# Interleaving 32 DRAM-to-DRAM weight conversions with the weight loads of an early projection, on eight cores

## The reference, cut to what matters

```python
xn = _layernorm(x)                                  # x: (4, 4096, 1024) f32
# attention-like part, D = 1024
magnitude = sigmoid(xn @ W_mag.T + b_mag) * 5.0
phi = random_phases * position * 0.01
mem_r = cumsum(magnitude * xn * cos(phi), axis=1)   # over all 4096 positions
mem_i = cumsum(magnitude * xn * sin(phi), axis=1)
acc_mag = cumsum(magnitude, axis=1)
q_off = xn @ W_q.T + b_q
... retrieved_r, retrieved_i from mem_r, mem_i, acc_mag, phi + q_off
context = concat([xn * cos_phi, xn * sin_phi, retrieved_r, retrieved_i])
attn = xn + (gelu(layernorm(context) @ W1.T + b1) @ W2.T + b2)
# feed-forward part, hidden width 4096
h = silu(xn @ w1.T * s1) * (xn @ w2.T * s2)
h = gelu(h @ h1_w.T * h1_s)                         # 4096 x 4096
h = gelu(h @ h2_w.T * h2_s)                         # 4096 x 4096
ffn = h @ w3.T * s3
return x + attn + ffn
```

## Time and profile before

| | us |
|---|---|
| median of two runs | 4950.73 |
| lowest and highest of them | 4926.67 and 4974.8 |
| the profiled execution | 4914.08 |
| its span, slowest core (core 1) | 4912.4 |
| spans of the eight cores | 4886.4 to 4912.4 |
| PE busy in the span | 3552.7 (72%) |
| DVE busy | 1630.9 (33%) |
| ACT busy | 925.0 (19%) |
| POOL busy | 399.9 (8%) |

### The profile page before, as it was taken

How to read it: one execution, slowest core, us unless ns; L and a number is a source line. 1 busy time by engine, 2 the same in 40 slices (tenths; PEclk the granted TensorE clock), 3 DMA queues, 4 the chain that set the end, 5 groups by cost and what they waited for, 6 DMA issues and landing times.

```text
span 4912.4 us, 46625 instructions; the slowest of 8 cores (4886.4 to 4912.4 us)
## 1 busy us (share of the span) xinstructions
PE 3552.7 (72%) x15504; PEld 1540.9 (31%) x15504; DVE 1630.9 (33%) x3773; ACT 925.0 (19%) x1243; POOL 399.9 (8%) x756
## 2 busy tenths in 40 slices
PE   3342002035879999878799997887999878899993
PEld 3220001002333444233244432332444333344441
DVE  2365667860023440430334405212443061100003
ACT  2111002220113331101133311011332200111000
POOL 0002001000120000001100000011000000210000
PEclk9997556557999999799899998998999899999997
DMA  2248994996684444376744444776444366844443
GB/s 75 77 107 101 110 120 55 110 109 117 113 137 131 148 149 151 69 142 115 118 146 152 152 131 79 149 114 122 150 153 154 95 113 136 124 145 152 154 140 79
DMA packets 125701, 600.90 MB, mean 122 GB/s; under 512 B 15867, under 2 KB 15900, under 8 KB 78364
## 3 DMA queue, kind: packets, MB, share of 16 engines
q0 software_dynamic: 108288, 545.31, 53.2%
q1 hardware_dynamic: 17180, 52.60, 3.3%
HBM read 866.29 MB, written 75.50 MB: 192 GB/s over the span
## 4 chain that ended last, share of the span: by engine, by line
PE 58%; DMA 19%; DVE 13%; issue 7%; ACT 2%; DVEq 1%; SPq 0%; POOLq 0%; ACTq 0%
PE ps L505 46%; DMA wstage<-w_t 9%; DMA wstage<-fw_t 5%; PE ps L985 2%; PE ps L976 2%; DMA xo<-pos_p 2%; PE ps L701 2%; PE ps L880 1%; DVE xo L473 1%; PE ps L870 1%; DMA xo<-x_fm 1%; DMA wstage<-h2b 1%; DMA wstage<-wq_t 1%; DVE big L477 1%; PE ps L331 1%
## 5 line engine op out<-in xcount | busy, mean ns | idle before, releaser
L505 PE MATMUL ps<-big,wstage 128*128 128x512 bf16 x12032 | 2691.9, 386 | 351.0 <-DMA wstage<-w_t 142.5
L505 PEld LDWEIGHTS ps<-big,wstage 128*128 128x128 bf16 x12032 | 1181.7, 99 | 1864.3 <-issue 524.2
L701 PE MATMUL ps<-xn_hi,wstage 128*128 128x512 bf16 x512 | 131.7, 425 | 472.4 <-DVE big L446 308.3
L995 DVE SCALAR_TENSOR_TENSOR big<-ps,svv_s,big 128x512 bf16<-128x512 f32 x128 | 96.1, 751 | 949.3 <-PE ps L985 949.3
L985 PE MATMUL ps<-xn_hi,wstage 128*128 128x512 bf16 x1024 | 246.0, 383 | 31.5 <-DMA wstage<-fw_t 28.0
L976 PE MATMUL ps<-xn_hi,wstage 128*128 128x512 bf16 x1024 | 243.5, 381 | 28.7 <-DMA wstage<-fw_t 21.9
L701 PEld LDWEIGHTS ps<-xn_hi,wstage 128*128 128x128 bf16 x512 | 54.2, 107 | 550.4 <-issue 503.5
L328 DVE COPY big<-ps 33x128 f32<-33x128 f32 (+1 forms) x36 | 11.8, 327 | 630.3 <-PE ps L880 528.5
L1037 ACT ACTIVATE big<-ps,svv_h2s 128x512 bf16<-128x512 f32 x128 | 88.0, 687 | 626.5 <-PE ps L505 626.1
L1059 DVE SCALAR_TENSOR_TENSOR obuf<-ps,svv_s,obuf 128x512 f32<-128x512 f32 x32 | 24.0, 750 | 544.5 <-PE ps L505 544.3
L880 PE MATMUL ps<-big,sel_b_sb 128*33 128x512 bf16 x128 | 73.1, 571 | 172.8 <-ACT big L876 144.2
(11 more groups left out here) (135 smaller groups left out, 2534.2 us busy)
## 6 DMA issues: line engine op xcount, KB each, us to landing
wstage<-h1b POOLq DMA_DIRECT2D x128, 1024.0 KB, 5.2
wstage<-h2b POOLq DMA_DIRECT2D x128, 1024.0 KB, 5.1
wstage<-w_t POOLq DMA_DIRECT2D x96, 1024.0 KB, 8.8
wstage<-fw_t POOLq DMA_DIRECT2D x256, 256.0 KB, 5.0
h1b<-h_t POOLq DMA_DIRECT2D x32, 1024.0 KB, 157.7
h2b<-h_t POOLq DMA_DIRECT2D x32, 1024.0 KB, 162.1
xo<-x_fm SPq DMA_DIRECT2D x48, 512.0 KB, 5.0
xo<-xp_fm SPq DMA_DIRECT2D x32, 512.0 KB, 3.5
```

What stands on the lines that cost most here:

```text
L505: last = e.matmul(psum[bank][:, 0:NMOV], wt_ap, mov_fn(k), start=(k == 0), stop=(k == K - 1))
L701: last = e.matmul(psum[bank][:, 0:NMOV], wt_ap, mov_xn(k), start=(k == 0), stop=(k == KD - 1))
L995: V(lambda e, m=m, bankB=bankB, yb=yb, ctxb=ctxb: e.scalar_tensor_tensor(out=big2[:, yb + m * M:yb + (m + 1) * M], in0=psum[bankB][:, 0:NM ...
```

## The change

The 32 conversions of `h1_t` are no longer issued in a row behind the wmag stage. A hook, called by `stream_projection` after every block of the wmag stage, issues one conversion after every second block. So 16 of them stand between the loads of the stage, and what is left is issued behind it. The conversions themselves, their data, their semaphore and the wait of their readers are the same.

```diff
-    def emit_wmag_prev(pp):
+    def emit_wmag_prev(pp, hook=None):
...
         stream_projection(dr["wmag_t"], D, D, mov_xnp_fn(pp),
-                          mov_xnp_bufs_fn(pp), evac_sigp)
+                          mov_xnp_bufs_fn(pp), evac_sigp, hook=hook)
...
+    _h1ch = []
+    for _m in range(32):
+        def _c(_m=_m):
+            dop("gpsimd", "CVT",
+                ap3(dr["h1b"], _m * 128 * DH, [[1, 1], [1, 128 * DH]]),
+                ap3(dr["h1_t"], _m * 128 * DH, [[1, 1], [1, 128 * DH]]))
+        _h1ch.append(_c)
+    _wg = [0]
+
+    def _wmag_hook():
+        _wg[0] += 1
+        if _wg[0] % 2 == 0 and _h1ch:
+            _h1ch.pop(0)()
     for pp in range(NP):
-        emit_wmag_prev(pp)
-    emit_convert(dr["h1b"], dr["h1_t"], DH, 0, 32, B_CVH1, "CVT")
+        emit_wmag_prev(pp, hook=_wmag_hook)
+    while _h1ch:
+        _h1ch.pop(0)()
+    B_CVH1.w = {"CVT": cnt["CVT"]}
```

## The result

The changed kernel is slower than before by the ratio 1.0119 (95% interval 1.0062 to 1.0176), within what the forecast called no change at 2%. Its profiled execution took 4992.59 us against 4914.08, with a span of 4991.0 on core 6 (4912.4 on core 1 before).

The account below looks back on a forecast made before the run. The wmag stage's end, gating emit_lite, three pos_p waits and the wait before the first W1 matmul were taken to bound the first 1150 us. +7 start, +85 stage, -31 waits gave +61 on 4927: 4988 us, range 4940 to 5055.

Parts of the forecast that it names:

- The first conversion: At about 3 us it holds up the first x load; the delay is carried to the wmag stage: +7 us.
- The stage: In the wmag stage, 14 conversions add 134 us of DMA work, 44 idle hide some: 90, taken as +85 us.
- Sigmoids ahead of sines on ScalarE: All 32 wmag sigmoids precede emit_lite's first sine on ScalarE, so the stage's end sets when emit_lite can run.
- The pos_p waits: In emit_lite, VectorE's waits of 19.93 and 11.43 us for pos_p loads go and 21.54 stays: 31 us saved.
- The last wait: 32.83 us before the first W1 matmul, weights queued behind h2 conversions; a shift of emit_lite's end passes through whole.
- The sum: +7 + 85 - 31 = +61 us, giving 4988 us from 4927, 1.2% over before.
- a pos_p load takes 8 turns of 4.5 us: Under conversions, SP's pos_p load has 8 data packets per engine, taking turns with the software queue: 36.24 us.
- The rival with starved x loads: In the wmag stage, x loads get few turns and VectorE reaches emit_lite late: +121 us, 5048 us; chance 0.10.
- The no-overlap rival: In the wmag stage, idle DMA time is not usable: +134 instead of +85, +110 in all, 5037 us; chance 0.12.
- Loads not held back: Weight loads pass the conversions, the wmag stage keeps its length: -4 us, 4923 us; chance 0.10.

Follow-up runs that it names:

- e1: Changed kernel with the conversion at the start of the program taken away; ratio 1.011 to the kernel before.
- e8: Changed kernel with a conversion behind every block of the wmag stage instead of every second; 5119.81 us in one execution, no ratio.
- e2: Changed kernel with a conversion behind every fourth block of the wmag stage, 7 between weight loads instead of 14; ratio 1.0055 to the kernel before.
- e3: Changed kernel with emit_wmag_prev(2) and (3) moved behind emit_lite(0) and (1), so 16 sigmoids precede the first sine; ratio 0.997 to the kernel before.
- e7: Changed kernel without the first conversion, emit_wmag_prev(2) and (3) behind emit_lite(0) and (1), emit_A0 behind emit_lite(1); ratio 1.0067 to the kernel before.
- e4: Kernel before with h1 and h2 conversions written in rows of 8 KB instead of 32 KB; 4997.0 and 4996.32 us, no ratio.

## Why the prediction was right

Its steps, in its own order, against the means of eight cores:

- *The first conversion, +7 of a range of 0 to 10.* 10.1 us, at the upper end of the range and not its middle: the conversion's own two packets, with nothing hidden. e1 shows it as a loss of its own.
- *The stage, +85 from 134 of added work less 44 idle.* 86.7. This was the step that carried the sum. It holds where its condition does, a queue that never runs dry: the DMA share went to 1.01, and for the 29 conversions of e8 the same sum gives 278 less 44, 234, where 228 were measured. With the 7 of e2 it would give 23 and 40.6 were measured at a DMA share of 0.74, so the rule is not one for every number of conversions.
- *Sigmoids ahead of sines on ScalarE.* Shown by e3, which keeps the conversions and moves only sigmoids: the loss of 1.2% goes away. The idle time before the first sine was to be over 100 us and was 80.8, since VectorE itself came later; x loads, which the sum had at no cost, took 41.4 us of VectorE's time, and all of it was hidden.
- *The pos_p waits, 31 us saved out of 52.9.* 33.0 of 55.1 came back (means of eight cores). One wait stayed (23.31), since its load still met the backlog; two went. The point that a load is hidden for its first 15 us kept this from being taken as 97 us, the length of the three loads in the chain.
- *The last wait, passed through whole.* 35.1 before, 36.9 after, so about 32 in all came back.
- *The sum, +61.* +64.9 at the first W1 matmul, and 1.19% by the ratio, where 61 of 4927 is 1.24%. The start was 3 us dearer than taken; the rest is within 2 us, term by term. The chances are not so tidy: 0.22 for slower is the 0.12 and 0.10 of the two rivals alone, and nothing is in it for the forecast's upper end, which the text names too.

One reading was right only in its product: that a pos_p load takes 8 turns of 4.5 us. In the kernel before, the queues of POOL (q0) and SP (q1) moved from 503 to 507 and from 507 to 511 us (packets, MB, share):

```profile
q0 software_dynamic: 16, 0.52, 113.5%
q1 hardware_dynamic: 16, 0.03, 10.8%
...
q0 software_dynamic: 32, 0.52, 119.9%
q1 hardware_dynamic: 32, 0.07, 16.1%
```

The 0.52 MB are 16 rows of 32 KB, one for each engine, and against it SP's queue got one row of the load for each engine, then two. The 8 rows came in five such groups between 498 and 523 us; the load was issued at 490.36, and the rest of its 36.24 us lies ahead of the first group and behind the last. The sum used the waits and not this product, so nothing in it hung on the slip. The rival with starved x loads did hang on it: with one packet for each turn it gave an x load 25 us, where 11.3 and 13.8 were measured.

The no-overlap rival falls by e2 (40.6 in the stage, not 67). Loads not held back falls by the stage itself. The starved x loads were true in part: they landed in a median of 11.3 and 13.8 us in the stage instead of 4.8 and 5.6, and VectorE came to emit_lite 48 us later. It did not decide, because the sigmoids were later still; e3 and e7 show it deciding as soon as the sigmoids are out of the way.

Of the two rules of the Trainium skill, that of "DMA: Bandwidth & Descriptors", section "Anatomy of one DMA", would have priced a conversion at an estimated 4.8 us, half of what it takes; e8, at 11 us for a block with one conversion, leaves no room for that. The section "Queues, rings and completion order" has an engine drain a whole packet of typically 9 to 17 descriptors per turn. Here the trace does not agree: a turn of the conversions' queue is one row of 32 KB, as just shown, and not the two rows that a conversion has on an engine. Had it been the whole of that share, shortening the rows in e4 would have changed nothing, and pos_p loads beside a full row landed in 17.9 us instead of 36.24 and 34.99.

What stays open: from the first W1 matmul to the end, the profiled execution of the changed kernel took 3782.4 us on its slowest core against 3765.7 before, with the same instructions; the mean granted clock there was 0.93 against 0.94. The ratio over many runs does not call for those 17 us, and no run here looked for their cause.

## What to carry to other kernels

A background transfer is priced by what stands behind it in its own queue, not by its bytes: the same conversion was nearly free beside the statistics (fifteen cost 2 or 3 us), cost 6 to 8 us between double-buffered loads, and 10 at the very start. Ask of each place whether the next load of the same queue has slack, and which in-order engine must finish the whole stage before somebody else can begin. And a transfer that only frees a late stretch is worth the wait that was not hidden, here 33 us, not its length in the chain.

## What the runs showed of the hardware

- Conversions DRAM to DRAM with a cast from f32 to bf16 moved 1 MB each in 9.6 us with all 16 engines busy, about 110 GB/s of written bytes. Written as rows of 8 KB instead of 32 KB they moved 3.15 MB in 30 us of a full queue, for 3.18.
- Beside a solid row of them, an engine moved one row of 32 KB of the conversions, then one or two rows of 2 KB of a load on SP's queue, and so on. A pos_p load took 36.24 us so, and 17.9 with rows of 8 KB; with rows of 32 KB an x load took 35.5, the one behind it 59.5.
- With 128 rows in a DMA instead of 32, POOL issued only 15 of them ahead and then stood still for 154 us (146 to 158 over both stops on the eight cores), so that a weight load behind them was issued at 746.53 instead of 434.68.
- SP's own issue of small loads took longer while a conversion was under way: 4.94 and 5.36 us for issues of 0.43 and 0.50, and 0.43 and 0.50 again with that conversion taken away (e1).
